# The softmax scaling of eight heads: one broadcast multiply on VectorE in place of eight on ScalarE

## The reference, cut to what matters

```python
def one_query(qs):
    return -jnp.sum(jnp.abs(qs[:, None, :, :] - k), axis=-1) * scale
...
a = jnp.concatenate([a, jnp.zeros((b, 1, t, h), a.dtype)], axis=1)
a = jax.nn.softmax(a, axis=1)[:, :t]
bf = jnp.einsum('bsdh,bshw->bdhw', a, vf)
bb = jnp.einsum('bdsh,bshw->bdhw', a, vb)
o = (bf + bb).sum(axis=2).reshape(b, t, d)
```

## Time and profile before

| what | value |
|---|---|
| median of 3 runs | 3578.32 us (3576.53 to 3587.6) |
| the profiled execution's own time | 3586.24 us |
| its span, first to last instruction | 3584.1 us |
| mean granted clock of TensorE | 0.983 of full speed |
| busy: PE / DVE / ACT / POOL | 91% / 87% / 75% / 80% of the span |

### The profile page before, as it was taken

The page is one execution under the profiler, slowest core; times in us unless marked ns, Lnnn a source line. Parts: engine busy times, 40 slices in busy tenths (PEclk is TensorE's granted clock), DMA queues, the critical chain, the costliest instruction groups (busy, mean ns, idle before and its releaser), DMA issues. The chain is left out here.

```text
span 3584.1 us, 78481 instructions
## 1 busy us (share of the span) xinstructions
PE 3276.2 (91%) x23008; PEld 2420.3 (68%) x23008; DVE 3115.8 (87%) x4449; ACT 2694.5 (75%) x4801; POOL 2851.3 (80%) x2724
## 2 busy tenths in 40 slices
PE   5899999999999999999999999999999999999886
PEld 4666667666667766667666677666677666677554
DVE  3889988898898898888899899899899899898884
ACT  1777877777877777777777777777777777777774
POOL 1788888888888888878888888888888888888874
PEclk8999999999999999999999999999999999999998
DMA  3777877787777787777887777787877787777874
GB/s 94 154 157 153 161 151 154 150 165 154 156 153 156 153 162 156 155 148 151 158 160 155 157 153 154 157 158 155 159 153 155 156 158 155 155 153 152 160 157 82
DMA packets 198692, 545.31 MB, mean 152 GB/s; under 512 B 68054, under 2 KB 132438, under 8 KB 145272
## 3 DMA queue, kind: packets, MB, share of 16 engines
q0 software_dynamic: 73728, 503.35, 71.0%
q1 hardware_dynamic: 124920, 41.40, 5.9%
HBM read 10.79 MB, written 2.10 MB: 4 GB/s over the span
## 5 line engine op out<-in xcount | busy, mean ns | idle before, releaser
L805 DVE TENSOR_REDUCE S<-psU 128x16 f32<-128x1024 f32 x2176 | 2603.5, 1217 | 295.7 <-PE psU L403 288.4
L403 PE MATMUL psU<-flat,kT 99*128 99x256 bf16 x16384 | 2315.7, 275 | 230.5 <-ACT absd L601 106.6
L601 ACT ACTIVATE absd<-psU 128x1024 f32<-128x1024 f32 x1920 | 1957.8, 1023 | 627.0 <-PE psU L403 604.7
L403 PEld LDWEIGHTS psU<-flat,kT 99*128 99x128 bf16 x16384 | 1489.2, 98 | 915.2 <-DVE S L805 235.7
L1072 POOL TENSOR_TENSOR absd<-absd 128x1024 f32<-128x1024 f32 (+2 forms) x512 | 1182.1, 2309 | 195.3 <-DMA absd<-absd 194.3
L1061 POOL DMA_DIRECT2D absd<-absd x512 | 453.9, 886 | 297.6 <-ACT absd L601 254.5
L1076 POOL TENSOR_TENSOR absd<-absd 128x512 f32<-128x512 f32 (+2 forms) x512 | 611.0, 1193 | 40.2
L1079 POOL TENSOR_TENSOR absd<-absd 128x256 f32<-128x256 f32 (+2 forms) x512 | 352.4, 688 | 40.1
L415 PE MATMUL psC<-c1in,w 128*128 128x384 f32 (+1 forms) x930 | 315.1, 421 | 0.6
L501 PE MATMUL psZ<-P,v 128*128 128x256 f32 x1024 | 311.2, 386 | 0.8 <-ACT P L719 0.8
L434 PE MATMUL psC<-c3in,w 128*128 128x128 f32 x1240 | 255.6, 289 | 4.5 <-DVE c3in L847 4.2
(11 more groups left out here) (166 smaller groups left out, 2187.0 us busy)
## 6 DMA issues: line engine op xcount, KB each, us to landing
absd<-absd POOLq DMA_DIRECT2D x416, 1024.0 KB, 7.8
flat<-qparts SPq DMA_DIRECT2D x3072, 8.0 KB, 4.0
absd<-absd POOLq DMA_DIRECT2D x64, 768.0 KB, 6.5
absd<-absd POOLq DMA_DIRECT2D x32, 512.0 KB, 4.8
xin<-in_x SPq DMA_DIRECT2D x32, 192.0 KB, 7.9
flat<-pattern SPq DMA_DIRECT2D x4, 768.0 KB, 10.8
out_h<-result SPq DMA_DIRECT2D x32, 64.0 KB, 5.9
w<-in_w SPq DMA_DIRECT2D x1, 1280.0 KB
```

Source lines behind the costliest of these rows:

```text
L403: mm = nc.tensor.matmul(psU[:, slot % PLACES, m], kT[0:ROWS + 3, b, m, :], flat[0:ROWS + 3, half % HALVES, :, lo:lo + BLOCK], start=True, ...
L601: nc.scalar.activation(absd[:, c % GROUPS, :, u], psU[:, slot % PLACES].rearrange("p (n a) s w -> p n (a s w)", n=2), ACT.Abs).then_inc(a_ ...
L805: nc.vector.tensor_reduce(S[:, b, hd, SB * c:SB * c + SB], psU[:, slot % PLACES].rearrange("p a s w -> p s a w"), AX.XY, ALU.add, apply_ab ...
```

## The change

The eight ACT instructions of a pass are gone, and so are their names in the table of ACT's steps. DVE gets one `tensor_tensor` right behind the reciprocal, behind a wait for it: it multiplies all of `P[:, :, 0, :]` (128 x 8 x 128, float32) by `rden`, whose column of a head is repeated 128 times by a broadcast access. PE's transposes now wait for that one step of DVE. The entries `scale=30, scale_len=8` stay in the table `AT_AT`, unused. No other step changes its slot.

```diff
 AT_PE = Steps("vf vb turna turnb pv")
-AT_ACT = Steps("vf vb exp0 exp1 exp2 exp3 exp4 exp5 exp6 exp7 scale0 scale1 scale2 scale3 scale4 scale5 scale6 scale7 turneda turnedb half tanh")
-AT_DVE = Steps("rden sum gate")
+AT_ACT = Steps("vf vb exp0 exp1 exp2 exp3 exp4 exp5 exp6 exp7 turneda turnedb half tanh")
+AT_DVE = Steps("rden scaled sum gate")
...
                             take_bank(at_act, AT_ACT.after(g, ("turneda", "turnedb")[n]))
-                            pe.wait_ge(at_act, AT_ACT.after(g, ("scale3", "scale7")[n]))
+                            pe.wait_ge(at_dve, AT_DVE.after(g, "scaled"))
...
-                for n in spread(slot, AT_AT["scale"], AT_AT["scale_len"], HEADS):
-                    if n == 0:
-                        act.wait_ge(at_dve, AT_DVE.after(g, "rden"))
-                    nc.scalar.activation(P[:, n, 0, :], P[:, n, 0, :], ACT.Copy, scale=rden[:, n:n + 1]).then_inc(at_act, 1)
...
                     nc.vector.reciprocal(rden[:, :], den[:, :]).then_inc(at_dve, 1)
+                    dve.wait_ge(at_dve, AT_DVE.after(g, "rden"))
+                    nc.vector.tensor_tensor(P[:, :, 0, :], P[:, :, 0, :],
+                                            rden[:, :].unsqueeze(2).broadcast_to([T, HEADS, T]),
+                                            ALU.mult).then_inc(at_dve, 1)
```

## The result

The changed kernel took 3614.62 us (median of 4 runs, 3612.14 to 3620.51), the kernel before beside it 3577.43 us (median of 4, 3571.75 to 3587.6). The ratio is 1.0099, 95% interval 1.0081 to 1.0116: about 1% slower, 37 us between the medians. The forecast was 3607 us, 29 us slower, with a range of 3588 to 3645 us. The profiled execution took 3613.26 us, 27 us more than the profiled one of before.

What follows compares the result with a forecast made beforehand. No engine alone was taken to set the time: PE came first in a ring of waits with DVE and ACT. First stretch 25 us plus second 4 us made 29 us, from 3578.32 to 3607 us; range 3588 to 3645 us.

Steps and rivals of the forecast that it cites:

- The multiply's price: Behind each pass's reciprocal: the multiply takes 1.22 us and lengthens DVE's queue by 1.175 us per pass.
- The first stretch: First pass, units 27 to 35: PE's unit 35 comes 0.80 us late, 31 times, 25 us in all.
- The rival of interference: First pass: GpSimd's L1076 delays the multiply by 0.93 us, 29 us more, 3636 us; second pass unaffected; chance 0.33.
- The likeliest case: Both stretches without interference: 29 us slower, 3607 us, own range 3595 to 3620 us; chance 0.47.
- Nothing that I find takes it back: First pass after unit 35: PE, DVE and ACT all stay late by the same 0.80 us.
- The second stretch: Second pass: ACT's relief lets DVE run without gaps, unit 109's reduction comes 0.12 us late, 32 times, 4 us.
- the forecast's walk: Second pass, unit by unit: PE 0.7 us late at unit 98, 0.4 at 103, 0.1 at 106 and 112.

Runs made afterwards that it cites:

- e5: Changed kernel with a one-input reduction of the same 128x1024 elements in the multiply's place, scaling left out; 3595.23 us, ratio 1.0051 to the kernel before.
- e1: Changed kernel with the multiply taken out, so no scaling on either engine; 3560.93 us, ratio 0.9945 to the kernel before.
- e2: Kernel before, ACT's eight scalings kept, with a 128x1024 DVE multiply of a scratch tile added behind the reciprocal; 3622.76 us, ratio 1.0118.
- e4: The change in the second pass only, ACT scaling as before in the first; 3585.63 us, ratio 1.0014 to the kernel before.

## Why the prediction was right

- **The multiply's price** was 1.175 us of DVE's queue, from DVE's 128x512 and 128x64 rows. It measured 1.22 us of record and 1.14 us to the next start, 0.035 us behind the reciprocal: right, for a multiply that nothing disturbs.
- **The first stretch** was put at 0.80 us. It is 0.80 us in each of the 7 iterations of 30 with an undisturbed multiply and 0.79 us in e5. In the median it is 1.36 us, since GpSimd holds the multiply up in most first passes. The step of the prediction that was mis-sized is this term: 25 us forecast, 31 x 1.36 = 42 us measured.
- **The rival of interference** was given 0.33 and 29 us more. The mechanism is there, as the long multiplies, GpSimd's own stretched records and e5 show together; its size is 17 us by e5, not 29. Two things made it smaller. A held multiply ends 1.08 us after GpSimd's operation and not 1.22, so it loses 0.80 us where 0.93 was reckoned. And I had taken the one iteration of the earlier trace rows, where GpSimd is ahead, for all. In 9 of 32 first passes DVE is ahead, or the two do not meet, and the multiply takes its 1.22 us. The second pass is undisturbed, as the earlier trace rows said. The Trainium skill (SBUF — State Buffer, Who interferes with whom) says that of such a pair the second to issue fully blocks until the first is done; both orders in this trace agree to within 0.14 us (2.02 us for DVE when second, 2.32 us in place of 1.27 for GpSimd when second). The likeliest case was thus forecast without a term that is real.
- **"Nothing that I find takes it back"** failed. Units 60 to 76 became 0.30 us shorter in every kernel with DVE work in the first pass, and by 0.10 us or less in the four without. Before, DVE waited there for GpSimd's queue. DVE before:

```profile
467.94 1.22 DVE L805 TENSOR_REDUCE S<-psU 128x16 f32<-128x1024 f32 x1 [0.20 <-PE psU L403]
469.41 0.42 DVE L816 TENSOR_REDUCE S<-absd 128x64 f32<-128x256 f32 x1 [0.25 <-POOL absd L1079]
469.75 0.61 DVE L842 SCALAR_TENSOR_TENSOR psC<-psC,mvc,ln1g 128x128 f32<-128x128 f32 x2
470.44 0.61 DVE L847 SCALAR_TENSOR_TENSOR c3in<-psC,rstdc,ln1b 128x128 f32<-128x128 f32 x2
470.97 2.34 DVE L805 TENSOR_REDUCE S<-psU 128x16 f32<-128x1024 f32 x2
```

and after, in the same iteration:

```profile
466.42 1.23 DVE L801 TENSOR_REDUCE S<-psU 128x16 f32<-128x1024 f32 x1 [0.19 <-PE psU L403]
467.56 0.41 DVE L812 TENSOR_REDUCE S<-absd 128x64 f32<-128x256 f32 x1
467.88 0.61 DVE L838 SCALAR_TENSOR_TENSOR psC<-psC,mvc,ln1g 128x128 f32<-128x128 f32 x2
468.40 0.60 DVE L843 SCALAR_TENSOR_TENSOR c3in<-psC,rstdc,ln1b 128x128 f32<-128x128 f32 x2
468.92 2.35 DVE L801 TENSOR_REDUCE S<-psU 128x16 f32<-128x1024 f32 x2
```

  From unit 71's reduction to unit 73's it is 3.03 us before and 2.50 us after: the wait for L1079 is gone, and so is the gap ahead of the step that needs GpSimd's `rstdc`. GpSimd, before and then after:

```profile
468.66 0.72 POOL L1079 TENSOR_TENSOR absd<-absd 128x256 f32<-128x256 f32 x1
...
466.32 0.72 POOL L1079 TENSOR_TENSOR absd<-absd 128x256 f32<-128x256 f32 x1
```

  L1079 ends 1.44 us after the start of unit 71's reduction before, and 0.62 us after it in the changed kernel. The 0.53 us are this iteration's; in the median it is 0.30 us. GpSimd's queue was late there before; the multiply makes PE and ACT late but not all of GpSimd's backlog, so GpSimd catches up by some of the delay. This gave 31 x 0.30 = 9 us back. That it is GpSimd's backlog is read from these rows and from which kernels show it; no kernel took it away by itself.
- **The second stretch** was put at +0.12 us with DVE full and ACT's relief spent on it. PE was late by 0.71 us at unit 98, 0.39 at 103, 0.12 at 106 and 0.06 at 112 in the median, as the forecast's walk had it (0.7, 0.4, 0.1, 0.1), and from unit 114 on not late at all: the last 0.06 us went into slack behind unit 112. 4 us forecast, 0 measured; the window shows DVE and ACT changed places, and e1, e2 and e4 show both halves of the balance.
- **Sum:** 25 + 4 = 29 us forecast. By the table 42 - 9 + 0 = 33 us, and 37 us measured. The errors are +17 us (the holding), -9 us (given back) and -4 us (the second stretch), and 4 us stay unexplained. That the total came this close to 29 us is in part luck: terms of opposite sign that the forecast did not have cancel by more than half. What was right without luck is the queue time of the multiply, what it costs where nothing holds it, and that ACT's relief pays for it in the second stretch and for nothing in the first.

## What to carry to other kernels

Work moved between engines is priced at the place where it lands and at the place that it leaves, each by what is waited for there: here ACT had 25% of its time free and DVE 13%, yet ACT's scalings were free in one pass and cost 0.7 of 2.35 us in the other. If the receiving engine's new operation reads two inputs from SBUF while GpSimd works on SBUF too, look at where GpSimd stands in each pass, not in one, and price the wait by GpSimd's operation rather than by the new one. And where one engine's work is in the way, first look whether it waits a little earlier in its own queue: moving the scalings of one pass within ACT's queue gained 0.4%, where handing those of both passes over to DVE lost 1%.

## What the runs showed of the hardware that I had not expected

An operation of DVE with two inputs in SBUF and one of GpSimd that reads SBUF exclude each other almost completely. The one that begins second, if only 0.03 us later, is recorded as begun, but ends as if it had started when the first ended, less 0.14 us. In every multiply that was held, the whole one (1.22 us alone) ended 1.08 to 1.10 us after GpSimd's operation, and the half one (0.69 us alone) 0.55 us after it. Four multiplies of the changed kernel that began in the last 0.02 to 0.08 us of a GpSimd operation were not lengthened at all. The start of a record is thus no sign that the work runs, and such a wait stands in no view of waits: it is seen only as a duration above the operation's least one.

Halving the multiply did not halve the extra time it was held (0.66 us in the mean against 0.54), and the longest hold turned a 1.22 us operation into 3.23 us. One input in SBUF does not suffice for it: neither the reduction of e5 nor L912 of before, with a write as long as the half multiply's, was ever lengthened.
